# More banks for the first row maxima of two attentions in a two-layer hybrid model

## The reference

```
x = x + attention_a(norm(x))     # 16 query heads, one shared key and value head, not causal
x = x + ffn(norm(x))             # both operands rounded to FP6 in blocks of 32
x = x + attention_b(norm(x))     # causal
x = x + ffn(norm(x))
x = x + latent_attention(norm(x))   # causal, keys and values from a latent of 32
x = x + experts(norm(x))            # top 2 of 8, and a shared one
x = x + attention_with_biases(norm(x))  # causal
x = x + experts(norm(x))

def attention(q, k, v):
    scores = q @ k.T / 8           # 1024 x 1024 per head
    return softmax(scores) @ v
```

## Time and profile before

| | us |
|---|---|
| median of 3 runs | 2677.7 |
| lowest and highest run | 2676.24, 2683.43 |
| profiled execution | 2670.4 |
| its span | 2668.7 |
| busy: TensorE, VectorE, GpSimd, ScalarE | 2469.3, 1681.9, 1241.7, 1213.4 |
| mean granted clock of TensorE | 0.953 of full |

### The profile page before, as it was taken

One profiled execution on the slowest core, in us unless ns is written; L12 is line 12 of the kernel. 1 busy time (PEld: TensorE's weight loads), 2 busy tenths in 40 slices (PEclk: granted clock), 3 DMA queues, 4 the chain that ended last, 5 costly groups with the idle time before them and its releaser, 6 DMA issues. The chain is left out here.

```text
span 2668.7 us, 48348 instructions
## 1 busy us (share of the span) xinstructions
PE 2469.3 (93%) x19929; PEld 1289.3 (48%) x19929; DVE 1681.9 (63%) x2159; ACT 1213.4 (45%) x1817; POOL 1241.7 (47%) x812
## 2 busy tenths in 40 slices
PE   4999999989999999999994799999879999999979
PEld 2344444334444444555552466666444555554545
DVE  2577767877765766666667467675445566666645
ACT  2444444535544545455441244444325455555432
POOL 2577777757775545555560000000004455555520
PEclk8899999999999999999995799999789999999979
DMA  4000000000000000000000100000000000000000
GB/s 108 1 1 1 1 1 1 1 1 1 0 1 10 1 1 1 1 1 1 1 1 0 33 3 3 3 3 3 1 1 1 1 1 1 1 1 1 1 1 17
DMA packets 19184, 14.07 MB, mean 5 GB/s; under 512 B 3090, under 2 KB 17811, under 8 KB 18836
## 3 DMA queue, kind: packets, MB, share of 16 engines
q1 hardware_dynamic: 18964, 10.97, 1.7%
HBM read 9.39 MB, written 1.57 MB: 4 GB/s over the span
## 5 line engine op out<-in xcount | busy, mean ns | idle before, releaser
L1370 POOL TENSOR_TENSOR sums<-sums,p 128x1024 f32<-128x1024 f32 (+3 forms) x384 | 816.6, 2127 | 369.5 <-PE ps L1026 328.9
L1208 DVE TENSOR_REDUCE half_max<-ps 128x2 f32<-128x1024 f32 (+3 forms) x384 | 442.2, 1152 | 331.7 <-PE ps L1007 319.0
L1110 ACT ACTIVATE p<-ps 128x1024 f32<-128x1024 f32 (+3 forms) x384 | 347.5, 917 | 222.1 <-PE ps L986 163.2
L983 PE MATMUL ps<-q,k 64*128 64x512 f32 (+3 forms) x1792 | 428.7, 557 | 0.0
L776 POOL TENSOR_TENSOR sums<-sums,p 128x1024 f32<-128x1024 f32 (+3 forms) x160 | 277.7, 1736 | 188.1 <-PE ps L544 170.9
L1026 PE MATMUL ps<-p,v 128*64 128x512 f32 (+3 forms) x1536 | 337.6, 554 | 0.0
L986 PE MATMUL ps<-max_row,pick 64*128 64x512 f32 (+3 forms) x896 | 328.4, 729 | 0.0
L1229 DVE RECIPROCAL inverse<-total 128x128 f32<-128x128 f32 x256 | 240.6, 943 | 15.6 <-ACT total L1148 12.0
L1007 PE MATMUL ps<-k_near,q_near 64*128 64x512 f32 (+2 forms) x896 | 200.4, 443 | 34.9 <-DVE half_max L1208 34.5
L1592 ACT ACTIVATE p<-ps 128x2048 f32<-128x2048 f32 (+1 forms) x80 | 136.6, 1708 | 162.3 <-PE ps L1495 90.8
L692 DVE TENSOR_REDUCE half_max<-ps 128x2 f32<-128x1024 f32 (+3 forms) x128 | 129.2, 1010 | 121.4 <-PE ps L525 106.9
(11 more groups left out here) (267 smaller groups left out, 3962.8 us busy)
## 6 DMA issues: line engine op xcount, KB each, us to landing
q_w<-in_wq SPq DMA_DIRECT2D x3, 512.0 KB
o_w<-in_wo SPq DMA_DIRECT2D x3, 512.0 KB
k_w<-in_wk SPq DMA_DIRECT2D x2, 512.0 KB
v_w<-in_wv SPq DMA_DIRECT2D x2, 512.0 KB
out<-x SPq DMA_DIRECT2D x4, 256.0 KB, 2.4
scratch<-in_wq_t SPq DMA_DIRECT2D x1, 512.0 KB, 5.4
scratch<-in_w_out SPq DMA_DIRECT2D x1, 512.0 KB, 7.5
gate<-in_gate SPq DMA_DIRECT2D x1, 320.0 KB
```

Of the source, the lines that this page charges most:

```text
L983: nc.tensor.matmul(out[:, head, 0:width], a.k[rows, owner(i) % 3, k * P:(k + 1) * P], a.q[rows, i % 3, s * BANK + lo:(s + 1) * BANK], star ...
L1110: act.activation(probabilities(g)[:, :, lo:BANK], score[g % 2][:, :, 0:BANK - lo], ACT.Exp)\
L1208: last = v.tensor_reduce(out, chunk_ps[:, :, 0:hi - lo], AX.X, ALU.max, negate=True)
L1370: pool.tensor_tensor(sums, sums, probabilities(g)[:, :, lo:BANK], ALU.add).then_inc(summed, 1)
```

## The change

Both functions get the same edit (that of `stream_phase` is shown where it differs in more than names). The buffer of a chunk becomes a function of its number. For c under 8 it rotates over banks 4 and 5, banks 0 and 1, banks 2 and 3; from c = 8 on it is banks 4 and 5 as before. Chunks 1 and 2 wait for nothing, chunks 3 to 7 for the maximum of the chunk three back (`maxed` at c - 2), later ones as before. The first two score steps wait until eight maxima are out. VectorE reads the same function's banks.

```diff
         score = [m.ps[:, 0:2, :], m.ps[:, 2:4, :]]
-        chunk_ps, mix, small = m.ps[:, 4:6, :], m.ps[:, 6, :], m.ps[:, 7, :]
+        mix, small = m.ps[:, 6, :], m.ps[:, 7, :]
+        chunk_banks = m.ps[:, 4:6, :], m.ps[:, 0:2, :], m.ps[:, 2:4, :]
+        EARLY = 8
+
+        def chunk_ps(c):
+
+            return chunk_banks[c % 3 if c < EARLY else 0]
+
...
                 if g >= 2:
                     pe.wait_ge(exped, g - 1)
+                else:
+                    pe.wait_ge(maxed, EARLY)
...
             def chunk(c):
                 i, (t, part, lo, hi) = c // NS, chunks[c % NS]
-                if c >= 1:
+                if c >= EARLY:
                     pe.wait_ge(maxed, c)
+                elif c >= 3:
+                    pe.wait_ge(maxed, c - 2)
...
-                    last = nc.tensor.matmul(chunk_ps[:, head, 0:hi - lo], a.q_near[rows, i % 2, t * P:(t + 1) * P],
+                    last = nc.tensor.matmul(chunk_ps(c)[:, head, 0:hi - lo], a.q_near[rows, i % 2, t * P:(t + 1) * P],
...
-                            last = nc.tensor.matmul(chunk_ps[:, head, at:at + HD], a.later[rows, half, :],
+                            last = nc.tensor.matmul(chunk_ps(c)[:, head, at:at + HD], a.later[rows, half, :],
...
-                last = v.tensor_reduce(out, chunk_ps[:, :, 0:hi - lo], AX.X, ALU.max, negate=True)
+                last = v.tensor_reduce(out, chunk_ps(c)[:, :, 0:hi - lo], AX.X, ALU.max, negate=True)
```

## The result

| | before | changed |
|---|---|---|
| median of 12 runs, us | 2676.97 | 2660.39 |
| lowest to highest, us | 2672.89 to 2685.18 | 2651.15 to 2671.05 |
| ratio, 95% interval | | 0.9939 [0.9923, 0.9955] |
| profiled execution, its span | 2670.4, 2668.7 | 2657.33, 2655.6 |

The ratio is worth 16.3 us (12.0 to 20.6). The forecast was 2659.9 us, 17.8 us less than before. Faster by more than 0.3%, as expected.

A forecast was written before the change was run, and what follows sets the result against it. TensorE bounds the long stages, so earlier starts carry through; its waits for VectorE's maxima slow the lead-ins. Stream 6.8 + a3 11.0 = 17.8 us off the 2677.7 us median gives 2659.9 us, range 2652 to 2669.

The forecast's parts named there:

- Stream lead-in, 6.8 us: Stream phase's first chunks: VectorE sets the pitch, so chunk 8 starts at 65.64 us instead of 72.47.
- The choice between 1.14 and 1.27 us for VectorE's pitch: Stream lead-in: spacing of successive row maxima; 1.14 us taken, gaining 6.8 us; 1.27 us would gain 5.9.
- a3, 11.0 us: Last attention's lead-in: waits removed and clock held full, chunk 8 at 1989.8 instead of 2000.75 us; range 6.25 to 13.2.
- Front: Last attention, causal chunks 0 to 3: 1.4 us instead of 4.6 up to the first value projection, 3.2 us earlier.
- Middle: Last attention, chunk 4 to the next pair's key projection: 6.0 us before, 3.05 us gained at the half clock.
- T + 2.15: Last attention at full clock: key projection 2.15 us after chunk 4 starts (T = 1984.7), at 1986.85 us.
- full clock at chunk 0, and lost at chunk 8: Last attention: gapless stretch keeps the clock full up to chunk 8; serial chunks 8 and 9 then run at half.
- half-clock rival: In a3 the clock falls anyway: gain 13.05 us, 2664.7 us; sign, clock 0.5 until the key projection; chance 0.27.
- Full clock to the end of both lead-ins: Rival: clock full up to the scores in stream phase and last attention; gain 22.4 us, 2655.3 us; chance 0.14.
- Nothing gained: Rival: maxima no closer together, or ACT and VectorE behind the chunks set both lead-ins; stays 2677.7 us; chance 0.10.
- Slower: Rival: at the stream phase's first scores the clock stays half for long; 2686 us or more; chance 0.02.

The follow-up runs named there:

- the ten-chunk kernel: The changed kernel with EARLY = 10 in place of 8 in both phases, so the rotation takes in chunks 8 and 9; measured 0.9906 and 0.991.

## Why the prediction was right

*Stream lead-in, 6.8 us.* Measured 6.91 in the first trace, and 6.9 in three others with three pairs and both with two (14.85 or 14.86 us each time, against 21.74 to 21.76). The choice between 1.14 and 1.27 us for VectorE's pitch was the only open term, and it reads 1.13: maxima of 1.23 us on ready chunks overlap at their ends by 0.1 us, as a maximum and the reciprocal behind it did. Nothing was lost between chunk 8 and the scores; alone the edit gave 0.0026, 7.0 us (2.9 to 11.0).

*a3, 11.0 us.* The forecast compared two executions that both enter at full, and for that no pair of traces with eight chunks exists. The profiled pair gave 6.8 us from the first key projection to the scores, 4.1 to 4.2 less than forecast, since one of the two entered at half. Both entered at half it is 11.4 us, near the forecast but for other reasons. By the whole time, a3 alone gave 7.2 us (3.8 to 11.0). Front: I took the chunks' own pitches at the full clock, 1.4 us up to the values; at half it was 1978.79 - 1976.42 = 2.37, and the ten-chunk kernel, at full, shows 1.43. Middle: from chunk 4 to the key projection I had T + 2.15, measured 1984.78 - 1982.46 = 2.32. Projections 1.90 apart, as at the full clock, and 1.06 to chunk 8.

*The step that was wrong: full clock at chunk 0, and lost at chunk 8.* The mechanism, that a stretch without gaps keeps the clock up, fits the two traces with ten chunks. The level at chunk 0, taken over from the trace of before, was wrong. In the changed kernel the clock did not hold, because it was not there: the three traces of kernels with the edit in a3 and eight chunks entered at half. It came up at the end of the gapless stretch, and it stayed up past chunks 8 and 9, whose serial wait I thought would cost it (the scores come 3.74 us behind chunk 8, not 5.47). So 3.8 us were lost ahead of chunk 0 (10.57 us against 6.77), another 2.0 us from chunk 0 to chunk 8, where the first four chunks and most of the first value projection ran at half (11.32 us against the 9.28 of the forecast), and 1.7 us were gained behind chunk 8. Together that is the 4.1 us by which a3's term fell short in the profiled pair. My sign for the half-clock rival, 0.5 at that place, reads 0.52 up to 1980.5 us and 1.00 from there on, so neither the forecast nor this rival describes the clock.

*The rivals.* Half clock throughout a3 did not happen with three pairs, but is just what both traces with two pairs show; its total, 2664.7 us, cannot be told from the measured one. Full clock to the end of both lead-ins came true in a3 behind the first value projection, and not in the stream phase, which reads 0.50 from 66.6 us to the scores. Nothing gained is excluded: each half of the change gains with an interval below 1. Slower: the clock came up 4.3 us behind the first scores, at 75.7 us (the pitch of the chunk there is that of the full clock), as it had at 81.5. The sentence of the Trainium skill (TensorE: Matmul & The Clock Gate, HAM oscillation), that double-buffering in PSUM gave one kernel no further gain, does not carry over to a lead-in: here the second pair gave 6.9 us, while the third gave nothing where VectorE was the bound.

The forecast total, 2659.9 us, lies 0.5 us from the median. With executions spread over 20 us that closeness is luck. The stream term is confirmed to 0.1 us; of a3's term the traced pair shows 6.8 of 11.0 us, and the whole time is too coarse to say more.

## What to carry to other kernels

Look for the pipeline's fill: a buffer that is enough when all engines are busy is a serial chain ahead of that, and banks that the next stage will own are free until then. Count the rotation to the point where the borrowed banks are really needed (ten here, not eight), since the first chunk behind it pays the full wait again. Where TensorE's clock is at half, removing short waits can be worth more than the waits: in a3, with both kernels entering at half, 5.4 us were waits and some 6 us clock. Compare two traces there only when the clock stood at the same level at the entry.

## What the runs showed that I had not expected

- Two lead-ins that differ by 0.4 us of waits can differ by 6 us. With two pairs of banks TensorE was busy 4.78 of 4.80 us in the chunk stretch and stayed at the half clock to the scores; with three it was busy 4.10 of 4.10 and came up, in three traces. The lead-ins are 21.04 and 15.06 us. That the small waits are the cause is not shown.
- The clock at the entry to a3 was full in two traces of the kernel before and two of the ten-chunk kernel, and half in that of the stream edit alone, in all three with eight chunks and three pairs, and in both with two pairs. It is worth 3.8 us. What sets it is open. It is not the code ahead of it alone: the kernel with the edit in a3 alone has the same code as the kernel before up to a3's chunks, and entered at half in its one trace. The margin is small: in the kernel before the clock was at half from 1969.5 to 1972.75 us and back at full by 1973, with the first projection at 1973.75.
- The work between the edited places, the same in every kernel here, takes one of two times, some 10 us apart. From the stream phase's last scores (1394.0 and 1397.2 us) to a3's first key projection (1965.9 and 1979.0) the two traces of the changed kernel took 571.9 and 581.7 us; those of the kernel before 573.6 and 584.3. The stretch below, first trace above second, shows one place where the granted clock differs, 0.66 and 0.60, and how much less was got through in the second (479 matmuls against 634). Another 3.3 us lie in the stream phase behind its first scores. This, and not the lead-ins (14.84 and 14.85, 15.06 and 15.23 us), is the spread between the two traced executions, and in a single pair it can hide or double what an edit gives.

```profile
1380.00:1520.00 140.00, 84.43 (x634) 50.22 (x634) 79.72 (x186) 35.00 (x57) 21.28 (x18) 0.66 0.07 16
1380.00:1520.00 140.00, 85.66 (x479) 48.62 (x477) 73.18 (x181) 32.74 (x59) 21.13 (x17) 0.60 0.07 15
```

- In the chunk stretch of the stream phase both traces of the changed kernel rose to full for a while and fell again: the chunks at 58.72, 59.85 and 60.98 us take 0.50 us, those at 62.12 and later 0.79 or 0.80. The mean of 0.78 in the row above is too high, since the view counts the time ahead of 58.7 us as full, where three chunks take 1.65 us, the pace of the half clock. The run with the stream edit alone, with the same stream phase, has 0.80 throughout.
